# Differential attention: floor, reciprocal and product of a batch's outputs placed on VectorE behind the mix of their step

## What is computed

```python
q  = heads(x @ Wq.T);  k1 = heads(x @ Wk1.T);  k2 = heads(x @ Wk2.T);  v = heads(x @ Wv.T)
s1 = q k1^T * SCALE;   s2 = q k2^T * SCALE              # causal
attn  = softmax(s1) - sigmoid(lambda_logit) * softmax(s2)
denom = maximum(sum(abs(attn)), 1e-6)
out   = (attn / denom) @ v
y     = out @ Wo.T
x     = x + layernorm(y)
```

## Time and profile before

| | |
|---|---|
| median of 3 runs | 2178.96 us (2178.22 to 2179.96) |
| the profiled execution's own time | 2184.45 us |
| span of its trace | 2182.7 us |
| attention's loop of 16 batches in the trace | about 50 to 755 us |
| one batch in the trace, 400.84 to 444.92 us | 44.08 us |

### The profile page before, as it was taken

The page is one execution under the profiler, slowest core; times in us unless marked ns, Lnnn a source line. Parts: engine busy times, 40 slices in busy tenths (PEclk is TensorE's granted clock), DMA queues, the critical chain, the costliest instruction groups (busy, mean ns, idle before and its releaser), DMA issues. The chain is left out here.

```text
span 2182.7 us, 42765 instructions
## 1 busy us (share of the span) xinstructions
PE 1899.5 (87%) x13162; PEld 1237.4 (57%) x13228; DVE 1654.4 (76%) x4446; ACT 1385.5 (63%) x4626; POOL 743.0 (34%) x683
## 2 busy tenths in 40 slices
PE   4999999999999748999986869999968376999998
PEld 2555555555555426777764447777745143666665
DVE  2888888888888758999974569999945656665666
ACT  2888888888888646888872248888833525333332
POOL 2555555555555443332321232333322312000000
PEclk9999999999999958999998979999989677999999
DMA  6000000000000000000001000000011000000000
GB/s 193 2 1 2 2 1 2 2 2 1 2 2 1 1 5 11 14 10 14 14 17 30 12 6 15 14 14 14 14 23 25 0 1 1 6 5 5 10 5 10
DMA packets 40722, 27.79 MB, mean 13 GB/s; under 512 B 23954, under 2 KB 33810, under 8 KB 40594
## 3 DMA queue, kind: packets, MB, share of 16 engines
q1 hardware_dynamic: 40594, 26.24, 4.7%
HBM read 10.51 MB, written 2.10 MB: 6 GB/s over the span
## 5 line engine op out<-in xcount | busy, mean ns | idle before, releaser
L408 ACT ACTIVATE a_E<-a_psS,a_nm 128x128 f32<-128x128 f32 (+1 forms) x1028 | 419.9, 429 | 25.9 <-DVE a_nm L240 23.7
L211 POOL TENSOR_SCALAR a_aT<-a_dT 128x384 f32<-128x384 f32 x256 | 307.1, 1200 | 323.8 <-PE a_psO L526 193.5
L240 DVE TENSOR_REDUCE a_nm<-a_psS 128x2 f32<-128x256 f32 (+1 forms) x514 | 261.5, 544 | 47.6 <-PE a_psS L493 46.9
L489 PE MATMUL a_psS<-a_kT,a_qm 32*128 32x128 f32 (+1 forms) x2064 | 242.0, 352 | 7.6 <-issue 3.7
L265 DVE SCALAR_TENSOR_TENSOR a_d<-a_E,a_cf 128x128 f32<-128x128 f32 (+1 forms) x512 | 217.0, 464 | 27.7 <-DVE a_cf L254 1.4
L408 ACT ACTIVATION_READ_ACCUMULATOR a_E<-a_psS,a_nm 128x1 f32 x1028 | 220.4, 214 | 0.0
L1587 ACT ACTIVATE mx_sl<-mx_psG 128x512 f32<-128x512 f32 x128 | 76.1, 597 | 198.7 <-PE mx_psG L1765 198.0
L417 ACT ACTIVATE a_dT<-a_psT 128x384 f32<-128x384 f32 x256 | 127.0, 496 | 93.4 <-PE a_psT L502 93.1
L827 POOL TENSOR_TENSOR b0rn<-b0ss,minus_half 128x16 f32<-128x16 f32 x36 | 107.1, 2976 | 222.0 <-DVE b0ss L863 222.0
L827 POOL TENSOR_TENSOR b1rn<-b1ss,minus_half 128x16 f32<-128x16 f32 x36 | 107.1, 2976 | 220.6 <-DVE b1ss L863 220.6
L489 PEld LDWEIGHTS a_psS<-a_kT,a_qm 32*128 32x128 f32 x2064 | 137.4, 187 | 58.1 <-issue 36.2
(11 more groups left out here) (304 smaller groups left out, 4532.3 us busy)
## 6 DMA issues: line engine op xcount, KB each, us to landing
b0v<-b0v SPq DMA_DIRECT2D x34, 128.0 KB, 2.3
b1v<-b1v SPq DMA_DIRECT2D x34, 128.0 KB, 2.3
out_dram<-mx_res SPq DMA_DIRECT2D x8, 256.0 KB, 2.3
f0z<-F SPq DMA_DIRECT2D x9, 128.0 KB
f1z<-F SPq DMA_DIRECT2D x9, 128.0 KB
f0z<-F SPq DMA_DIRECT2D x9, 127.0 KB
f1z<-F SPq DMA_DIRECT2D x9, 127.0 KB
wqk<-in_wqkv_dram SPq DMA_DIRECT2D x2, 512.0 KB, 4.6
```

Source lines behind the costliest of these rows:

```text
L211: pool.tensor_scalar(aT[:, s, :], dT[:, s, :], 0.0, None, ALU.max).then_inc(positived.sem, 1)
L240: ins = dve.tensor_reduce(nm[:, s, t, :], psS[:, s, :, (0, P)[t]:(P, 384)[t]], axis=AX.X, op=ALU.max, negate=True)
L408: ins = act.activation(E[:, s, m, c0:c1], psS[:, s, m, c0:c1], ACT.Exp, bias=nm[:, s, t, m:m + 1], accum_out=Z[:, p, h, t, m:m + 1])
L489: pe.matmul(psS[:, s, m, c0:c1], qm[rows, p, a, r, t * P:(t + 1) * P], kT[rows, p, a, 0:c1 - c0], start=(t == 0), stop=False)
```

## The change

In steps 3 and 5, floored, denominators and normalise_o leave their places among maxima, inverse and coefficient, and all three stand behind the step's mix. No instruction is added or removed, none changes its size, and the waits of each are the same calls.

```diff
                     for s in range(H):
                         nxt = (pair, half + (s + 1) // H, (s + 1) % H)
+                        maxima(*nxt, 0)
+                        maxima(*nxt, 1)
+                        k = inverse(pair, half, s)
+                        k = coefficient(pair, half, s, k)
+                        mix(pair, half, s, k)
                         if s in (3, 5):
                             floored(pair, half, s // 2 - 1)
-                        maxima(*nxt, 0)
-                        if s in (3, 5):
                             denominators(pair, half, s // 2 - 1)
-                        maxima(*nxt, 1)
-                        k = inverse(pair, half, s)
-                        if s in (3, 5):
                             normalise_o(s // 2 - 1)
-                        k = coefficient(pair, half, s, k)
-                        mix(pair, half, s, k)
                         if s == 4:
```

## The result

The changed kernel has a median of 2170.65 us over 6 runs (2168.82 to 2172.02) against 2181.83 us for the kernel before over 6 runs on the same occasions (2178.22 to 2184.55). The ratio is 0.9950, with a 95% interval of 0.9937 to 0.9962: 0.4 to 0.6% faster. The forecast was 2169.7 us with 2163.5 to 2178.5, faster with 0.68.

What follows compares the result with a forecast made beforehand. TensorE, busy 42.66 of 44.08 us a batch, was taken as the bound, with gains only in its stalls. 16 batches × 0.58 = 9.3 us off the 2178.96 us median gave 2169.7 us, range 2163.5 to 2178.5.

Steps and rivals of the forecast that it cites:

- The bound and the stalls: TensorE bounds the loop; its stalls at turn(3) and turn(5) cost 0.60 us each, 1.20 us a batch.
- The two waits of the floor: VectorE idle before the floor in steps 3 and 5, waiting for TensorE's transposes of OT; 0.40 us in step 5.
- Step 3: VectorE's mix(3) starts at 404.38 instead of 405.37, turn(3) no longer waits, and TensorE gains 0.56 to 0.60 us.
- The block at 0.70, dearer by 0.27: Floor, reciprocal and product together on VectorE cost 0.70 us, spread out 0.43; hidden in step 3, exposed in step 5.
- The holds: VectorE is held about 0.27 us when an instruction with SBUF inputs starts together with GpSimd's positive part.
- The second hold: In step 5, mix(5) and GpSimd's positive part start together, costing VectorE 0.27 us, new against before.
- The first hold: In step 4, the positive part of head 3 meets VectorE's coefficient; a hold of 0.27 us is kept there.
- the row of 405.37: Mix in the kernel before, started inside GpSimd's positive part, took its 0.75 us; cited against a full lock.
- Steps 5 and 6: mix(6) starts at 413.30, turn(6) at 414.10 with a new stall of 0.37 us; 0.58 us gained.
- The ceiling of 0.95: At turn(6), what TensorE's own order would gain in a batch if nothing held it: 0.95 us.
- One sign: TensorE's busy time per batch was to stay the same.

Runs made afterwards that it cites:

- x_otfirst: Kernel before, VectorE's order untouched, TensorE's transposes of OT put ahead of the numerators in steps 2 and 4; batch 43.42 us, ratio 0.9950.
- x_inter: Kernel before, floor and reciprocal each one place later among the maxima, product unmoved, all ahead of the mix; batch 43.48 us, ratio 0.9968.
- x_step3: Kernel before with only step 3's three instructions moved behind its mix, step 5 left as it was; batch 43.41 us, ratio 0.9949.
- x_spread: Changed kernel, but in step 5 only the floor stays behind the mix; reciprocal and product are spread into step 6; batch 43.17 us, ratio 0.9941.
- x_step5: Kernel before with only step 5's three instructions moved behind its mix; batch 43.52 us in ten batches, 43.86 in five; ratio 0.9964.
- x_nopos4: Changed kernel without GpSimd's positive part of head 4, its semaphore still raised; batch 43.18 us, ratio 0.9933.
- x_bnopos4: Kernel before without GpSimd's positive part of head 4, its semaphore still raised; batch 44.04 us, one run.

## Why the prediction was right

*The bound and the stalls.* Right. The two waits of the floor are gone, turn(3) has no stall, and x_otfirst and x_inter show that it was the wait and not the place. One size was low: a stall costs more than the 0.60 us. Behind a stalled turn(3) the next scores start 0.47 us later (406.17 to 406.64), behind an unstalled one 0.42 (397.21 to 397.63). So what two stalls cost is 2 × 0.65 = 1.30 us a batch, not 1.20.

*Step 3.* Right to 0.01 us for VectorE. Put on the forecast's time (8.35 us later, mix(2) starting at 402.27 and at 393.92), mix(3) starts at 404.38 as forecast, the floor at 405.04 as forecast. maxima(5) start at 405.76, forecast 405.77; the block ends just as the scores come, so it is hidden there. TensorE gained more than forecast: the scores behind turn(3) start at 405.98 on this time instead of 406.64, 0.66 us earlier, where the prediction had 0.56 to 0.60 and went on with 0.56, for which it names no row. x_step3 confirms the size with its 0.67.

*The block at 0.70, dearer by 0.27.* Right: 0.72 and 0.70 were measured, and x_spread won 0.31 us by breaking up the exposed one. The prediction weighed a rule of the Trainium skill against this (VectorE: DVE Perf Modes, "The DRAIN you can't avoid": a semaphore between following instructions costs nothing extra). It concluded from it that a block would cost no more than the spread form; that is out by 0.3 us for the three. Whether the semaphore has a share in this is not shown: no run takes it away, and the three could cost more merely because each has to wait for the result of the one before it with nothing between them.

*The holds.* The second hold, a coin by the prediction's own word, fell as it was called: GpSimd at 401.54, mix(5) at 401.56 with 1.02 us. That is luck in part: x_step5 shows the same pair of instructions fall both ways in one trace. x_nopos4 and x_bnopos4 show that this was its cause and 0.30 us its price. The first hold was in the coefficient of head 4 (398.54, 0.10 us behind the GpSimd start at 398.44), which took 0.42 us instead of its usual 0.22, so 0.20 instead of the 0.27 that were counted. No mix in these traces took more than 1.08 us, so none was held for the 1.16 us of a positive part. This speaks against the rule of the Trainium skill (SBUF — State Buffer, "SBUF: two separate sides": the first of the two has the port pair for its whole instruction) here, as the row of 405.37 did.

*Steps 5 and 6.* Right, a little too careful. mix(6) was forecast for 413.30 and came at 413.19: maxima(7) were 0.08 early, and from them to mix(6) are 1.42 us in both kernels (412.06 to 413.48, 403.42 to 404.84), not the 1.45 that was carried over from step 4; turn(6) forecast with a stall of 0.37 us, measured 0.30; the gain 0.58, measured 0.60 a batch, and a batch of 43.5, measured 43.48. The gain comes so close although TensorE won about 0.10 more in step 3, which fits that VectorE's way to turn(6) sets it, as the prediction had it. The ceiling of 0.95 was given without its working; the best kernel here, x_spread, came to 0.91. One sign did not come: TensorE's busy time of a batch was to stay the same and went from 42.66 to 42.82 us. The profile models the ends of matmuls, and what makes the 0.16 is open.

*What the prediction didn't see.* It took both halves of the change as needed. x_step3 shows that the second was not: when step 3 is mended, the transposes of step 4 come early enough for the floor of step 5 in its old place, but for 0.08 us. The price of the second block and its hold then outweigh what it saves, by 0.07 us a batch.

*From batches to the median.* 16 × 0.60 = 9.6 us, and the traces show 9.1 for the whole loop. The measured medians differ by 11.2 us, with 8.3 to 13.7 by the interval (0.9962 and 0.9937 of 2181.83). The forecast subtracted from the 2178.96 us of the first three runs; the median of before over six runs was 2181.83, because three more near 2184 us came in. The forecast's closeness to 2170.65, 0.95 us, is therefore in part luck; the length of the batch is the better test of it.

## What to carry to other kernels

A wait on an engine that works in order costs what stands behind it, not the work it guards: find the row with idle time before it, and see whether the instructions behind it had their data already. Then move the waiting instruction only as far as the wait needs, and no group of short dependent instructions into a block where the engine is the limit: between longer independent ones the three cost 0.43 us here, as a block 0.70. When two stalls follow each other on one chain, mend the first and look again before mending the second.

## What the runs showed of the hardware

VectorE's mix takes 0.75 us when no GpSimd instruction starts near it. When it starts shortly behind a start of GpSimd's positive part, it takes longer, the more so the closer the starts: 1.02 us at 0.02 us behind (401.56 behind 401.54), 0.98 at 0.07 in x_inter (398.81 behind 398.74), 0.82 at 0.22 in the kernel before (413.48 behind 413.26), and again 0.75 at 0.63 (405.37 behind 404.74). The product, which has one of its two inputs in PSUM, takes its 0.29 us even at 0.06 behind (404.80 behind 404.74). When GpSimd starts 0.30 us behind the mix, as in x_step5, either of the two pays, in batches whose rows agree to 0.01 us up to there: GpSimd takes 1.47 instead of 1.17 us, or the mix 1.08 instead of 0.75. At 0.36 behind, GpSimd pays 0.24 us (396.39 behind 396.03, 1.41 us). So in these traces a pair of starts within some tenths of a microsecond costs up to 0.33 us, never the whole instruction, and at 0.30 us starts that differ by less than 0.01 us went with a different payer. That moves a batch by 0.3 us, as much as half of the gain here.

That TensorE's matmuls got short at 42 us in one execution and at 51 us in another, with the same work before, was not expected either; what sets that moment stays open.
